# Value products of each odd chunk moved ahead of the outputs, the next norm's transposes behind them

## What is computed

```python
def _linear_attention(x, Wq, Wk, Wv, Wo):
    Q = _phi((x @ Wq).reshape(b, t, H, DH)).transpose(0, 2, 1, 3)   # _phi(x) = elu(x) + 1
    K = _phi((x @ Wk).reshape(b, t, H, DH)).transpose(0, 2, 1, 3)
    V = (x @ Wv).reshape(b, t, H, DV).transpose(0, 2, 1, 3)
    S = jnp.cumsum(jnp.einsum('bhti,bhtj->bhtij', K, V), axis=2)
    z = jnp.cumsum(K, axis=2)
    num = jnp.einsum('bhti,bhtij->bhtj', Q, S)
    den = jnp.maximum(jnp.einsum('bhti,bhti->bht', Q, z), EPS_DEN)[..., None]
    return (num / den).transpose(0, 2, 1, 3).reshape(b, t, H * DV) @ Wo
```

## Time and profile before

| | |
|---|---|
| median of 3 runs | 806.81 us (806.21 to 807.58) |
| the profiled execution's own time | 806.17 us |
| its span in the profile | 804.4 us |
| PE busy | 788.3 us, 98% of the span |
| DVE / ACT / POOL busy | 71% / 69% / 44% |
| pair 0 to pair 15 in the trace | about 195 to 582 us |
| PE share of the chain that ended last | 83% |
| TensorE's granted clock, mean | 0.998 of full speed |

### The profile page before, as it was taken

The page is one execution under the profiler, slowest core; times in us unless marked ns, Lnnn a source line. Parts: engine busy times, 40 slices in busy tenths (PEclk is TensorE's granted clock), DMA queues, the critical chain, the costliest instruction groups (busy, mean ns, idle before and its releaser), DMA issues.

```text
span 804.4 us, 27852 instructions
## 1 busy us (share of the span) xinstructions
PE 788.3 (98%) x11719; PEld 674.9 (84%) x11719; DVE 571.8 (71%) x1332; ACT 557.9 (69%) x1005; POOL 351.1 (44%) x281
## 2 busy tenths in 40 slices
PE   6999999999999999999999999999999999999997
PEld 5788878788889898899898998988888788888886
DVE  8958485556978789787888878799699663638210
ACT  4877868868665666665666565667678787878775
POOL 3988979881001010010100101010255797979784
PEclk9999999999999999999999999999999999999999
DMA  7002111201001001010100101102034220201011
GB/s 249 14 14 79 53 54 40 78 1 55 16 3 53 0 1 52 0 53 0 38 15 0 53 0 41 51 0 67 15 106 118 67 65 14 66 13 40 9 45 28
DMA packets 56700, 33.53 MB, mean 42 GB/s; under 512 B 1984, under 2 KB 55232, under 8 KB 56640
## 3 DMA queue, kind: packets, MB, share of 16 engines
q1 hardware_dynamic: 56640, 32.79, 14.0%
HBM read 22.29 MB, written 10.49 MB: 41 GB/s over the span
## 4 chain that ended last, share of the span: by engine, by line
PE 83%; ACT 8%; DVE 5%; issue 2%; POOL 1%; DMA 0%; SPq 0%; ACTq 0%; DVEq 0%; POOLq 0%
PE ps L728 37%; PE ps L915 18%; PE ps L687 8%; PE ps L809 6%; PE ps L978 4%; PE ps L989 4%; PE ps L1005 3%; ACT ee L1321 3%; PE ps L961 3%; ACT rr L1322 2%; DVE ol L1788 2%; ACT vt L1343 1%; ACT kf L1353 1%; POOL alB L1911 1%; ACT oh L1363 1%
## 5 line engine op out<-in xcount | busy, mean ns | idle before, releaser
L1321 ACT ACTIVATE ee<-ps 128x512 f32<-128x512 f32 x128 | 78.2, 611 | 90.0 <-PE ps L915 60.0
L1911 POOL TENSOR_TENSOR alA<-full,ahA 128x512 fp32r<-128x512 f32 x82 | 110.9, 1366 | 54.7 <-DVE ahA L1497 24.7
L2004 POOL TENSOR_TENSOR as<-as,power 128x4 f32<-128x4 f32 x16 | 19.0, 1189 | 265.2 <-DVE as L1706 235.5
L1911 POOL TENSOR_TENSOR alB<-full,ahB 128x512 fp32r<-128x512 f32 x84 | 110.7, 1330 | 22.5 <-ACT ahB L1200 7.7
L1489 DVE SCALAR_TENSOR_TENSOR full<-ps,sc,gate 128x512 f32<-128x512 f32 x64 | 46.6, 747 | 98.9 <-PE ps L728 69.7
L728 PE MATMUL ps<-ahA,wh 128*128 128x512 f32 x288 | 113.3, 393 | 1.4 <-DVE wh L1532 1.4
L728 PE MATMUL ps<-ahB,wh 128*128 128x512 f32 x288 | 113.3, 393 | 0.0
L728 PE MATMUL ps<-alA,wh 128*128 128x512 f32 x288 | 112.2, 390 | 0.0
L728 PE MATMUL ps<-alB,wh 128*128 128x512 f32 x288 | 112.2, 390 | 0.0
L1199 ACT ACTIVATE full<-ps,sc 128x512 f32<-128x512 f32 x86 | 59.6, 693 | 29.3 <-PE ps L728 20.0
L1322 ACT ACTIVATE rr<-ps 128x512 f32<-128x512 f32 x128 | 78.8, 616 | 0.0
(11 more groups left out here) (191 smaller groups left out, 2173.9 us busy)
## 6 DMA issues: line engine op xcount, KB each, us to landing
wst<-in_ternary SPq DMA_DIRECT2D x5, 512.0 KB, 8.0
stage<-in_attn SPq DMA_DIRECT2D x4, 512.0 KB, 3.9
xlnA<-x_scratch SPq DMA_DIRECT2D x8, 256.0 KB, 2.8
axr<-x_scratch SPq DMA_DIRECT2D x8, 256.0 KB, 3.1
yx_scratch<-ay SPq DMA_DIRECT2D x8, 256.0 KB, 2.3
xs_scratch<-axs SPq DMA_DIRECT2D x8, 256.0 KB, 2.4
xlnA<-yx_scratch SPq DMA_DIRECT2D x8, 256.0 KB, 2.8
xlnB<-yx_scratch SPq DMA_DIRECT2D x8, 256.0 KB, 2.9
```

The costliest lines, as they stand in the source:

```text
L1321: nc.scalar.activation(ee[k][:, :], src[:, :], ACT.Exp).then_inc(*X["act"].step(f"e_{name}"))
L1911: return nc.gpsimd.tensor_tensor(dst, src, hi.bitcast(F32), ALU.subtract)
```

## The change

In the first half of each pair the two value products V come directly behind the two key products K, ahead of I and O, and N comes behind O, directly ahead of WO. In the last pair, which has no N, V moves ahead of the outputs in the same way. ACT's queue follows: the copies of V come ahead of the copy of N. DVE's and SP's queues are as they were. Since the ring is dealt in the order of the code, V now has banks 6 and 7 and N bank 0, where N had 6 and V had 7 and 0. In the last pair V had 6 and 7 before as well.

```diff
@@ attention_plan (which bank each product gets) @@
                 for h in range(2):
                     phi(turn(), f"K{o}.{h}")
+                for h in range(2):
+                    values(turn(), o, h)
                 outputs(e)
                 if not last:
                     norm(turn(), hh + 1)
                     split(hh + 1)
-                for h in range(2):
-                    values(turn(), o, h)
                 first = turn() if last else None
                 bank = turn()
@@ PE, pair(hh) @@
                 for h in range(2):
                     token_major("K", o, h)
+                for h in range(2):
+                    token_major("V", o, h)
                 outputs(e)
                 norm(hh + 1)
-                for h in range(2):
-                    token_major("V", o, h)
                 if hh:
                     output_projection(hh - 1)
@@ PE, last_pair(hh) @@
                 for h in range(2):
                     token_major("K", o, h)
-                outputs(e)
                 for h in range(2):
                     token_major("V", o, h)
+                outputs(e)
                 output_projection(hh - 1)
@@ ACT, attention_act @@
                     if last:
                         table(ACT.Gelu)
-                    else:
-                        norm(hh + 1)
                     for h in range(2):
                         values(o, h)
+                    if not last:
+                        norm(hh + 1)
```

## The result

The changed kernel takes **815.68 us** (median of 4 runs, 814.87 to 815.94) against 807.19 us for the kernel before, measured beside it (4 runs, 806.21 to 807.88). The ratio is 1.0104, with a 95% interval of 1.0092 to 1.0116: 8.5 us slower. The profiled execution took 815.94 us, with a span of 814.1 us.

The account below looks back on a forecast made before the run. PE was taken as the bound, busy 788.3 of 804.4 us. Loop 7.4, pair 0 0.3 and last pair 0.55 gave 8.3 us on 806.2, so 814.5; median 0.6 higher, stated as 815.0 us, range 812.0 to 817.5.

Parts of the forecast that it names:

- The total: Whole kernel: 815.0 us as measured median, 1.0% slower, within 812.0 to 817.5 us.
- V.0's wait: First half of each loop pair: V.0's bank waits for am a, so PE idles 0.55 us.
- V's restart: V.0 starts from a drained array after its wait: 0.11 us more in its first distance.
- The rival without restarts: V.0 stalls for am a but matmul restarts are free: 811.8 to 813.5 us, chance 12%.
- The rule of the Trainium skill: At V.0, a weight load hidden during the wait would save 0.11 us, giving about 813.4 us; the sum did not use it.
- The cover of O's wait: First half of a pair: V covers the wait for am b ahead of O, a gain of 0.13 us.
- WO behind N: First half of a pair: WO pays the first fp32r matmul behind transposes, 2.98 us for 2.89.
- The loop's sum: K.0 to KT takes 8.81 us against 8.28: +0.53 us a pair, 7.4 us for 14 pairs.
- Pair 0 and the last pair: Pair 0: KT.1 waits for `ahf`, 0.3 us. Last pair: V.0 waits for am a, 0.55 us.

Follow-up runs that it names:

- the half of the change that has no new wait in the loop: Against the kernel before, only N moved behind V, with V still behind the outputs: 807.89 us, ratio 1.0008.
- masks-first kernel: Changed kernel with DVE's masks of each even chunk ahead of the additions to the state: 806.21 us, ratio 0.9991 to the kernel before.
- a further bank choice: Changed kernel with DVE's masks ahead of the state additions, and N of pair 0 alone in the bank WO leaves unused: 806.22 us, ratio 0.9984.
- the same edit on DVE: DVE's masks of even chunks ahead of the state additions: 806.21 us in the changed kernel, 823.83 us in the kernel before.

## Why the prediction was right

*The total.* Forecast 815.0 us in 812.0 to 817.5; measured 815.68 us, a difference of 8.5 us to the kernel before where the sum had 8.3.

*V.0's wait.* Forecast 0.55 us idle, V.0 starting 2.03 us behind K.0; measured 0.50 and 1.99. The 0.08 us from DVE's end to PE's start were 0.06. am a kept its place behind K.0, 1.93 us (1.95 in pair 5 of before), so DVE's chain moved with PE and did not compound. One sentence of the prediction is wrong by its own rows: PE is not 1.5 us ahead of the masks when it leaves K (that is how long K takes), but 0.5 us ahead of am a's end and 1.1 us ahead of am b's. The sum did not use the 1.5. That the wait causes the cost is shown from both sides: with am a earlier it vanishes, at unchanged order on PE, and with the half of the change that has no new wait in the loop the time is the old one within 0.2%.

*V's restart.* Forecast 0.11 us more in the first distance; measured 0.34 us to the next start in the changed kernel and 0.23 without the wait. The rival without restarts falls. The timeline of the weight loads (PEld) shows V.0's load in pair 5 of the changed kernel:

```profile
320.83 0.19 PEld L915 LDWEIGHTS ps<-wah,ahh 128*128 128x128 f32 x1 [0.77 <-DVE am L1748]
```

The load starts at 320.83 with its matmul, behind the wait, and not ahead of it. Without the wait, in the masks-first kernel, it starts at 317.87, 0.22 us ahead of its matmul at 318.09.

The rule of the Trainium skill that the prediction weighed ("TensorE: Matmul & The Clock Gate", section "Part 2: What happens when you issue a matmul") is that PE can pull a weight load ahead of matmuls still in flight. The rows agree with it in the stream of matmuls, by those 0.22 us, and show no such gain behind a wait.

*The cover of O's wait.* Forecast a gain of 0.13 us; O follows I after 0.99 us and lasts 1.05. The masks-first kernel, which keeps this gain and has no wait for am a, is 0.14 us a pair faster than the kernel before.

*WO behind N.* Forecast 2.98 us, measured 2.96.

*The loop's sum.* 0.51 us a pair against 0.53. For pairs 2 to 14 that is 6.6 us for 6.9.

*Pair 0 and the last pair.* Pair 0 was forecast at 0.3 us and gave 0.30, by the wait named; a further bank choice takes it away. The last pair, to its scores, was forecast at 0.55 and gave 0.62 in one pair of executions and 0.54 in the other.

*What the sum lacked.* Pair 1 was counted as one of the fourteen at 0.53 us. Its first half lost 1.38 us in one pair of executions (14.43 less 13.05) and 0.84 in the other (14.14 less 13.30). Beyond the 0.53, a first-pass loss of 0.3 to 0.9 us had no term in the sum. It made up for the 0.3 us that the loop's term was too large, so the nearness of 8.3 and 8.5 is in part luck, of a few tenths of a microsecond. The parts measured here add up to 8.9 us in the first pair of executions and to 8.3 in the second; the spans of these executions differ by 9.7 and 7.8 us, so 0.8 us more in the first pair and 0.5 us less in the second lie outside these parts.

## What to carry to other kernels

When a product is moved ahead in a full queue, ask first which buffer it will write, since a ring that is dealt in code order moves the buffers with it: the wait for the old reader moves ahead too, and everything behind it in the queue pays. Then set the order of the feeding engine by what the new order asks for first; the same edit on DVE here was worth 9.5 us with one order of PE and cost 17 us with the other. Count the changes of tile shape in a reordering, since each cost a tenth or two of a microsecond here, where the engine has no idle time.

## What the runs showed of the hardware that was not expected

An excursion from 64x65 matmuls to 128x512 ones and back cost about 0.36 us beyond the matmuls, at the one place where it was tried: 0.11 ahead of the first large one, 0.11 in its first distance, 0.10 before the small ones, 0.04 in their start. I had expected 0.21 of it.

PE's first pass through a stretch of code can lose time that later passes do not: 0.7 to 2.2 us in the first half of pair 1, partly the same in each execution, and again in pair 2 when the loop starts there. The view books it partly to "issue", in the scores, and partly to whoever released a semaphore last, as the 1.03 us to `ahf`; a wait that shows in one pass of a loop alone is therefore not to be read as that engine's.
